# A gated feed-forward kernel: the last batch kept whole, and the down products of the batch before it moved behind the last up product

## The reference, cut to what matters

```python
scale = cond @ norm_w.T + 1.0
h = x * (scale[:, None, :] * rsqrt(mean(x * x, -1) + EPS))     # x: 8 x 512 x 512
u = h @ up_w.T                                                 # 4096 columns
val, gate = split(u, 2, -1)
h = val * gelu(gate)                                           # 8 x 512 x 2048
hq = act_quant(h)      # s = 127 / max|h| of a token; clip(round(h * s), -128, 127) / s
wq = weight_quant(down_w)                                      # ternary, one scale
out = hq @ wq.T + x
```

## Time and profile before

| what | value |
|---|---|
| median of 3 runs (855.2 to 855.95) | 855.53 us |
| span of the profiled execution | 853.5 us (853.54 by the clock of the windows) |
| TensorE matmul busy | 825.9 us, 97% of the span |
| VectorE busy | 520.1 us, 61% |
| ScalarE busy | 218.2 us, 26% |
| mean DMA share | 12.6% of 16 engines |
| mean granted TensorE clock | 0.996 |

### The profile page before, as it was taken

The page is one execution under the profiler, slowest core; times in us unless marked ns, Lnnn a source line. Parts: engine busy times, 40 slices in busy tenths (PEclk is TensorE's granted clock), DMA queues, the critical chain, the costliest instruction groups (busy, mean ns, idle before and its releaser), DMA issues.

```text
span 853.5 us, 11741 instructions
## 1 busy us (share of the span) xinstructions
PE 825.9 (97%) x4497; PEld 432.6 (51%) x4497; DVE 520.1 (61%) x746; ACT 218.2 (26%) x345; POOL 9.7 (1%) x17
## 2 busy tenths in 40 slices
PE   5998989999999999999999999999999999989995
PEld 4555544544444444444445444444444444866872
DVE  6799966843578324863368435783258633963837
ACT  5887833210042002311032100420023110110110
POOL 1000000000000000000000000000000000000000
PEclk9999999999999999999999999999999999999998
DMA  5822001001200002001020012000020010202000
GB/s 177 339 89 74 25 29 48 1 8 43 83 16 0 25 25 98 0 0 40 21 86 0 13 36 92 6 0 25 25 98 0 0 46 15 87 2 75 1 26 25
DMA packets 18935, 38.35 MB, mean 45 GB/s; under 512 B 1496, under 2 KB 2016, under 8 KB 18400
## 3 DMA queue, kind: packets, MB, share of 16 engines
q1 hardware_dynamic: 18896, 38.02, 12.6%
q10 hardware_dynamic: 16, 0.00, 0.0%
HBM read 29.63 MB, written 8.39 MB: 45 GB/s over the span
## 4 chain that ended last, share of the span: by engine, by line
PE 87%; DVE 10%; issue 1%; DMA 1%; ACT 1%; SPq 0%; DVEq 0%
PE Y L741 12%; PE V L718 12%; PE V L720 12%; PE V L719 12%; PE G L718 12%; PE G L720 12%; PE G L719 12%; DVE h L522 2%; PE X L683 1%; DVE mpart L498 1%; DVE h L484 1%; DVE whl L469 1%; DVE h L528 1%; DVE inv_w L455 1%; DMA xin<-in_x_dram 1%
## 5 line engine op out<-in xcount | busy, mean ns | idle before, releaser
L484 DVE SCALAR_TENSOR_TENSOR h<-V,c_all,g 128x512 f32<-128x512 f32 (+2 forms) x144 | 99.3, 690 | 292.2 <-PE V L720 272.2
L366 ACT ACTIVATE g<-G,c_all 128x512 f32<-128x512 f32 (+1 forms) x144 | 91.9, 638 | 496.1 <-PE G L720 483.6
L718 PE MATMUL V<-xT,wT 128*128 (+2 forms) x576 | 204.7, 355 | 3.0 <-DVE h L484 3.0
L718 PE MATMUL G<-xT,wT 128*128 (+2 forms) x576 | 204.7, 355 | 1.7 <-ACT dT L405 1.7
L720 PE MATMUL G<-xT,wT 128*128 (+2 forms) x576 | 204.7, 355 | 0.0
L719 PE MATMUL G<-xT,wT 128*128 (+2 forms) x576 | 204.7, 355 | 0.0
L720 PE MATMUL V<-xT,wT 128*128 (+2 forms) x576 | 204.7, 355 | 0.0
L719 PE MATMUL V<-xT,wT 128*128 (+2 forms) x576 | 204.7, 355 | 0.0
L741 PE MATMUL Y<-dT,q 128*128 128x512 f16 x480 | 108.5, 379 | 0.0
L718 PEld LDWEIGHTS V<-xT,wT 128*128 128x128 f16 x576 | 56.4, 98 | 55.8 <-DVE h L484 4.1
L720 PEld LDWEIGHTS V<-xT,wT 128*128 128x128 f16 x576 | 56.4, 98 | 54.3
(11 more groups left out here) (110 smaller groups left out, 413.3 us busy)
## 6 DMA issues: line engine op xcount, KB each, us to landing
wst<-in_L_cond_up_w_dram SPq DMA_DIRECT2D x16, 512.0 KB, 4.0
xin<-in_x_dram SPq DMA_DIRECT2D x8, 1024.0 KB, 5.5
xres<-in_x_dram SPq DMA_DIRECT2D x28, 256.0 KB, 4.1
out_dram<-whl SPq DMA_DIRECT2D x28, 256.0 KB, 2.0
q<-in_L_cond_down_w_dram SPq DMA_DIRECT2D x2, 1024.0 KB, 9.8
xin<-in_x_dram SPq DMA_DIRECT2D x4, 256.0 KB, 4.9
dw<-in_L_cond_down_w_dram SPq DMA_DIRECT2D x1, 1024.0 KB, 10.1
h<-in_L_cond_down_w_dram SPq DMA_DIRECT2D x1, 1024.0 KB, 10.0
```

The costliest lines, as they stand in the source:

```text
L366: act.activation(g[:, s % 2, u.cols], G[s % 2][:, u.cols], ACT.Gelu, scale=c_of(u.b, s, 1))\
L484: dve.scalar_tensor_tensor(out=h_tiles(u, s, 1).rearrange("p n t -> p (n t)"), in0=V[s % 2][:, u.cols], scalar=c_of(u.b, s, 0), in1=g[:, s ...
L718: pe.matmul(bank[:, u.cols], high, xT_tile(u.b, 0, k, u.cols), start=(k == 0), stop=False)
```

## The change

The last batch is one unit `FINAL` of 512 tokens, like the others. Batch 6 (`BEFORE`) is quantised beside FINAL's steps 0 to 7 as before, but its four down tiles come after FINAL's last up product. FINAL's `transpose_max` stands behind the first of these tiles and its `spread_scale` in the middle of the second. VectorE quantises FINAL pair by pair and puts batch 6's four outputs between (`STAGED_AT`); of the 8 pairs it rounds the four with an even index, and ScalarE the four with an odd one, each in two Copy activations: add the magic number in place (`add_magic`), then subtract it and write f16 (`q_round` on ScalarE). FINAL's quantised values go to `q_end`, a part of `wT` that is free by then, and its dequantisation factors to `dq_end`. TensorE multiplies pairs 0 to 5 down over all four tiles as they come, and pairs 6 and 7 tile by tile (`BY_TILE_FROM`), into the banks V0, V1, G0 and G1.

```diff
-    DOWN_AFTER_IN_A = {11: 0, 12: 1, 13: 2, 14: 3}
-    DOWN_AFTER_IN_B = {9: 0, 11: 1}
+    STAGED_AT = {0: 0, 1: 1, 3: 2, 5: 3}
+    BY_TILE_FROM = 6
...
-        HALF_A = Unit(LAST, LAST, 0, TT // 2)
-        HALF_B = Unit(LAST, LAST + 1, TT // 2, TT // 2)
+        FINAL = Unit(LAST, LAST, 0, TT)
+        BEFORE = Unit(LAST - 1, LAST - 1, 0, TT)
+        q_end = wT[:, :, :, :].rearrange("p s v n -> p (s v n)")[:, 0:FT * T]
...
+        LASTY = [V[0], V[1], G[0], G[1]]
...
+            def add_magic(u, i):
+                pair = h_tiles(u, 2 * PAIR_ORDER[i], 2)
+                act.wait_ge(q_clipped, PAIRS * u.i + (i + 1))
+                act.activation(pair, pair, ACT.Copy, bias=MAGIC).then_inc(magic_added, 1)
+
+            def q_round(u, i):
+                act.wait_ge(magic_added, (i + 1) // 2)
+                act.activation(q_of(u, i), h_tiles(u, 2 * PAIR_ORDER[i], 2), ACT.Copy, bias=-MAGIC)\
+                   .then_inc(q_ready_act, 1)
...
-            for u in (HALF_A, HALF_B):
-                for s in range(FT):
-                    gelu(u, s)
+            for s in range(FT):
+                gelu(FINAL, s)
+            for i in range(1, PAIRS, 2):
+                add_magic(FINAL, i)
+                q_round(FINAL, i)
...
+            quant_scale(BEFORE)
+            for s in range(FT):
+                hidden(FINAL, s)
+                behind(BEFORE, s)
+            quant_scale(FINAL)
             for i in range(PAIRS + 1):
                 if i < PAIRS:
-                    q_scale(HALF_B, i)
-                if i > 0:
-                    q_round(HALF_B, i - 1)
+                    q_scale(FINAL, i)
+                if i in STAGED_AT:
+                    staged_out(BEFORE, STAGED_AT[i])
                 if i < PAIRS:
-                    q_clip(HALF_B, i)
-            for t in HALF_B.tiles:
-                y_out(HALF_B, t, V[t % 2], xin[:, t, :], ytail[:, t, :])
+                    q_clip(FINAL, i)
+                if i > 0 and i % 2:
+                    q_round(FINAL, i - 1)
+            dve.wait_ge(x_loaded, 16 * B)
+            for t in range(TT):
+                y_out(FINAL, t, LASTY[t], xin[:, t, :], ytail[:, t, :])
...
+            down_tile(BEFORE, 0)
+            transpose_max(FINAL)
+            down_tile(BEFORE, 1, range(0, FT // 2))
+            spread_scale(FINAL)
+            down_tile(BEFORE, 1, range(FT // 2, FT))
+            down_tile(BEFORE, 2)
+            down_tile(BEFORE, 3)
+
+            def final_pair(i, t):
+                s = 2 * PAIR_ORDER[i]
+                down(FINAL, t, LASTY[t], (s, s + 1), 2 * PAIR_ORDER[0], 2 * PAIR_ORDER[-1] + 1)
+
             for i in range(PAIRS):
-                pe.wait_ge(q_ready, PAIRS * HALF_B.i + i + 1)
-                s = 2 * PAIR_ORDER[i]
-                for t in HALF_B.tiles:
-                    down(HALF_B, t, V[t % 2], (s, s + 1), 2 * PAIR_ORDER[0], 2 * PAIR_ORDER[-1] + 1)
+                if i % 2:
+                    pe.wait_ge(q_ready_act, i // 2 + 1)
+                else:
+                    pe.wait_ge(q_ready, PAIRS * LAST + i // 2 + 1)
+                if i < BY_TILE_FROM:
+                    for t in range(TT):
+                        final_pair(i, t)
+            for t in range(TT):
+                for i in range(BY_TILE_FROM, PAIRS):
+                    final_pair(i, t)
```

More of the change, by code:

```diff
@@ L158, in h_tiles, with dq_of, q_of @@
             return h[:, bass.ds(at, n * T)].rearrange("p (n t) -> p n t", t=T)[:, :, u.cols]
+        def dq_of(u):
+            return dq_end if u is FINAL else dq
+        def q_of(u, i):
+            s = 2 * PAIR_ORDER[i]
+            to = q_end if u is FINAL else q[:, :]
+            return to[:, s * T:(s + 2) * T].rearrange("p (n t) -> p n t", t=T)
         def xT_tile(b, part, k, cols=slice(0, T)):
@@ L538, in y_out @@
                 dve.wait_ge(y_psum, TT * u.b + (t + 1))
[L539 removed]
+                dve.scalar_tensor_tensor(out=stage, in0=bank[:, :], scalar=dq_of(u)[:, t:t + 1], in1=res,
                                          op0=ALU.mult, op1=ALU.add).then_inc(y_done, 1)
@@ L547, in behind, with staged_out @@
                     q_round(prev, s)
[L548 to L557, removed]
+                if prev is not BEFORE and s - 1 in DOWN_AFTER:
+                    staged_out(prev, DOWN_AFTER[s - 1])
+            def staged_out(u, t):
+                use = 32 * u.b + 16 * (t // 2 + 1)
+                dve.wait_ge(xres_loaded[t % 2], use)
+                dve.wait_ge(ystage_free[t % 2], use)
+                y_out(u, t, Y[t % 2], xres[:, t % 2, :], ystage[:, t % 2, :])
             for i in range(2):
@@ L738, in down @@
             def down(u, t, bank, steps, first, last):
+                of = q_end if u is FINAL else q
                 for s in steps:
-                    mm = pe.matmul(bank[:, :], q[:, s * T + t * P:s * T + (t + 1) * P], dT[:, s, :],
+                    mm = pe.matmul(bank[:, :], of[:, s * T + t * P:s * T + (t + 1) * P], dT[:, s, :],
                                    start=(s == first), stop=(s == last))
@@ L749, in behind, with down_tile @@
                     spread_scale(prev)
[L750 to L753, removed]
+                if prev is not BEFORE and s in DOWN_AFTER:
+                    down_tile(prev, DOWN_AFTER[s])
+            def down_tile(u, t, steps=range(FT)):
+                if 0 in steps:
+                    pe.wait_ge(q_ready, PAIRS * u.i + PAIRS)
                     if t >= 2:
-                        pe.wait_ge(y_done, TT * prev.b + (t - 1))
-                    down(prev, t, Y[t % 2], range(FT), 0, FT - 1)
+                        pe.wait_ge(y_done, TT * u.b + (t - 1))
+                down(u, t, Y[t % 2], steps, 0, FT - 1)
             pe.wait_ge(consts_ready, 1)
@@ L804, in _ @@
             pe.wait_ge(xlo_ready, KT * B)
[L805 to L813, removed]
-            for i in range(PAIRS):
-                pe.wait_ge(q_ready, PAIRS * HALF_B.i + i + 1)
-                s = 2 * PAIR_ORDER[i]
-                for t in HALF_B.tiles:
-                    down(HALF_B, t, V[t % 2], (s, s + 1), 2 * PAIR_ORDER[0], 2 * PAIR_ORDER[-1] + 1)
+            for s in range(FT):
+                up(FINAL, s, 1)
+                if s == 0:
+                    transpose_max(BEFORE)
+                up(FINAL, s, 0)
+                behind(BEFORE, s)
+            down_tile(BEFORE, 0)
[6 more added lines that the diff above has]
+            def final_pair(i, t):
+                s = 2 * PAIR_ORDER[i]
+                down(FINAL, t, LASTY[t], (s, s + 1), 2 * PAIR_ORDER[0], 2 * PAIR_ORDER[-1] + 1)
+            for i in range(PAIRS):
+                if i % 2:
[8 more added lines that the diff above has]
+                    final_pair(i, t)
 _INS = ["x", "cond_256", "L0_cond_norm_w", "L0_cond_up_w", "L0_cond_down_w"]
```

21 lines of the change are left out of this document (6 added, 15 removed).

## The result

| | before | with the change |
|---|---|---|
| median | 855.74 us (855.2 to 857.94, 4 runs) | **843.11 us** (842.3 to 843.74, 4 runs) |
| ratio, 95% interval | | 0.985 [0.9836, 0.9865] |
| span of the profiled execution | 853.54 us | 841.99 us (its own time 843.58) |

The account below looks back on a forecast made before the run. TensorE's column work bounds the middle, its waits at the end are winnable. U at 806.28, plus 27.6 to the last 16 matmuls, plus 7.26, gives 841.1; plus 1.99 around the span, 843.1 us (range 841.9 to 846.8).

Parts of the forecast that it names:

- U: The moment FINAL's last up product is issued on TensorE; predicted at 806.28 us.
- the burst: TensorE's last 16 down matmuls; predicted to start at U + 27.6 us, after 2.0 us of idling.
- stretch: From the last batch's first matmul to the span's end; predicted 118.7 instead of 131.1 us.
- Step 1: FINAL's up products on TensorE: 6.16 + 15 x 5.18 = 83.86 us from its first matmul.
- Step 2: Handover from last up product through transposes and spread_scale to the first q_scale: 6.44 us.
- Step 3: VectorE's chain of scales, clips, rounds and outputs, from first scale to start of last clip: 18.22 us.
- Step 4: ScalarE's last pair: two activations of 1.05 us plus handovers, 2.23 us, bounds 2.17 to 2.41.
- Step 5: TensorE's readiness in the tail: waits some 0.4 us for output 0, idles 2.0 us before the last 16 matmuls.
- Step 6: The end: last 16 matmuls, last output and store, together 7.26 us.
- Rival 1: Clock falls in TensorE's last gap: up to 3.45 us more, 844.0 to 846.6 us; chance 0.34.
- Rival 2: ScalarE or VectorE a tenth slower working side by side in the tail: 845 us; chance 0.09.
- Rivals 3 and 4: 3: clock falls at tail's head, stays down, 869 us, chance 0.03. 4: semaphore holds batch 6's downs, 853.5, 0.02.

Follow-up runs that it names:

- e3: Changed kernel with ScalarE rounding pairs 1, 3, 5 and 6 (6 and 7 exchanged between ScalarE and VectorE): 841.98 us.
- e4: Changed kernel with ScalarE rounding pairs 1 to 6 and VectorE only 0 and 7: 841.65 us.
- e8: Changed kernel without 15 of the 16 matmuls of batch 6's tile 3 (its output is wrong): 843.29 us.
- e7: Changed kernel with two more Copy activations in place between the two of the last pair, lengthening TensorE's last gap: 847.81 us.
- e5: Changed kernel, last batch whole and ScalarE rounding, but batch 6's down tiles left beside its up products: 854.16 us, ratio to before 0.9968.
- e2: Changed kernel with all 8 roundings on VectorE, none on ScalarE: 844.22 us.
- e1: The changed kernel once more, no edit: 842.61 us.
- e10: The changed kernel once more, no edit, in five rounds: 842.94 us.
- e6: Kernel before, halves kept, with HALF_A's two down tiles moved behind HALF_B's last up product: 853.64 us, ratio 0.9954.
- e9: e4 with batch 6's output 0 moved on VectorE ahead of the last batch's first scale: 840.14 us, ratio to before 0.9818.

## Why the prediction was right, step by step

| term | predicted | measured |
|---|---|---|
| last batch's first matmul to U | 83.86 | 807.29 - 723.51 = 83.78 |
| U to the first scale | 6.44 | 813.55 - 807.29 = 6.26 |
| first scale to the last clip | 18.22 | 831.75 - 813.55 = 18.20 |
| last clip to the burst | 2.92 | 834.77 - 831.75 = 3.02 |
| burst to the end of the span | 7.26 | 841.99 - 834.77 = 7.22 |
| stretch | 118.70 | 118.48 |
| time around the span | 1.99 | 843.58 - 841.99 = 1.59 |
| U | 806.28 | 807.29 |

**Step 1** held. That U itself was 1.0 us late is not the change's: the last batch began 1.09 us later (723.51 against 722.42), as the head of the program varies by. With that the profiled execution was expected at 844.2 and took 843.58; the median hit to 0.1 us is partly luck, since the head alone moves it by 1 us.

**Step 2** was 0.18 too long. `spread_scale` started at U + 5.62 where I had 5.75: my own rows add up to 3.46 + 0.48 + 1.73 = 5.67, and the four transposes took 0.43 us. The first scale then came 0.64 us behind it, not 0.69.

**Step 3** was right to 0.02 us, and it is the step that carries the forecast: start-to-start distances, taken apart for dependent and independent neighbours, over the listed order. Durations added up would have given 4 x 1.21 + 4 x 1.21 + 4 x 0.74 + 7 x 0.69 + 3 x 0.69 = 19.5 instead of 18.2.

**Step 4**: an activation takes 1.06 us, between my two bounds; the Trainium skill's formula (ScalarE: Activation LUTs, "What ACT_TABLE_LOAD costs") gives 1.04 as an estimate, 2% under. My upper bound used 0.84 ns a column with no row beside it; ScalarE's Gelus of 512 and 256 columns, 0.69 and 0.47 us in the trace of before, give 0.86. From ScalarE to TensorE it was 0.14 us, where I had 0.05; that is nearly all of the 0.10 us by which this term was short. e3 and e4 show the term for what it was: the price of having the last link on the slower route.

**Step 5**: the waits were 0.34 and 1.93 us, I had 0.4 and 2.0. e8 showed that this slack is real, by removing 3.2 us of work to no effect.

**Step 6** held to 0.04 us.

**Rival 1** (0.34) didn't come about in any of three profiles of this kernel; e7 showed that it exists, and what it costs, in a gap of 4 us. By the rule of the Trainium skill (TensorE: Matmul & The Clock Gate, "Part 1: The HAM clock gate") recent activity keeps the clock up; the traces agree in that TensorE had just idled ahead of every fall shown here, but it didn't fall behind every such gap: 1.76 us idle never did it, 2.54 and 2.61 us did it in some profiles and not in others. Of the single executions without a trace this can't be said. **Rival 2** did not appear: VectorE's durations in company are those of before (0.69, 1.21), and ScalarE's Copy stayed within my bounds. **Rivals 3 and 4** did not appear either: the clock was 1.00 throughout the tail, and the outputs stand between the pairs as listed.

Where I said what is saved, I named idle time ahead of the first down matmul, the bursts at half clock and the stalls at both half boundaries, without sizes. The time was right, but two of these three were misread. The bursts at half clock cost the kernel before nothing in the end, since VectorE bounded its tail: by pairs 5 and 6 TensorE was at full clock and waiting for VectorE again. At most the two transposes of the scales ahead of them (0.69 us) were slower for it.

```profile
846.53 1.04 PE L741 MATMUL V<-dT,q 128*128 128x512 f16 x4 [0.23 <-DVE q L533]
847.80 1.90 PE L741 MATMUL V<-dT,q 128*128 128x512 f16 x8 [0.23 <-DVE q L533]
```

And the long stall was not at a boundary but inside HALF_A:

```profile
756.13 0.28 PE L718 MATMUL V<-xT,wT 128*128 128x256 f16 x1 [2.61 <-DVE h L484]
```

At the two boundaries TensorE idled for 1.09 and 0.18 us ahead of the transposes of `m`. In the changed kernel it has no such stall: it is busy for all of the 83.78 us from 723.51 to U. e5 gives the one split that was measured: 11.1 us by the move, 1.5 us by whole batch and ScalarE together. The two parts of that 1.5, the whole batch and ScalarE's help, were not taken apart with the downs in place; e2 prices ScalarE's part at 0.8 us with the downs moved.

## What to carry to other kernels

Before shortening a serial tail (here quantise, multiply, store), look for work of the stage ahead that only has to be done some time, and put it there: 64 matmuls that cost 13.6 us beside a full TensorE lengthened a tail bound by VectorE by 2.5 us, and that by their four outputs on VectorE more than by themselves. Then look at the last link alone: here ScalarE's help was worth its time everywhere but behind the last clip, where its 3.02 us counted in full; exchanging two equal tasks gave 1.5 us. And order a list so that an instruction is not followed at once by its own successor; to forecast such a chain, add start-to-start distances, not durations.

## What the runs showed of the hardware that I had not expected

**The same gap drops the clock in one execution and not in another.** In the first batch, with the same code up to there, TensorE waits 2.54 us once (idle by the rows, as in all of this section). In e3's profile and in e1's, by the same windows:

```profile
82.20:85.70 3.50, 3.50 (x10) 1.25 (x9) 2.47 (x7) 0.00 (x0) 0.00 (x0) 0.51 0.45 154
```

```profile
82.20:85.70 3.50, 3.37 (x29) 1.93 (x27) 2.60 (x7) 1.40 (x2) 0.00 (x0) 1.00 0.42 154
```

In e3 the clock was 0.51 over that stretch, in e1 1.00. All fourteen profiles have this gap; in four of them (e2, e3, e5, e10) the clock fell behind it, in ten it did not. The gap in step 10 of HALF_A, 2.61 us, did the same (1.00 in the profile of before, 0.52 in e6). A single gap of 1.76 us never did it in what was seen, nor did e8's one of 2.35, and e7's 3.94 did. But shorter gaps in a row can: in the tail of the kernel before the clock fell at 836.6, in the second of two gaps of 1.49 and 1.13 us with two transposes between them. The last batch kept whole also removes the gap in HALF_A, and with it one such chance.

**The fall may come after the gap is over.** In e7 all of the 4 us of idle time passed at 1.00, and the matmuls behind it paid. The first batch of e3 does the same: work began again at 81.15, and its matmuls went from 0.22 to 0.43 us apart only from 82.2 on.

**An independent instruction on VectorE starts before its neighbour has ended**, by 0.07 to 0.09 us (in e9 the scale at 814.42 takes 1.21 us, and the output behind it starts at 815.56), and a dependent one 0.03 us after. A clip of 0.69 us is followed by another pair's round after 0.60 us (816.22 and 816.82 in e9), by its own after 0.72 (829.02 and 829.74). Over the chain that is more than 1 us.
